# Weighted sums of two key tiles behind each other, and a ring of twelve exponential tiles

## The reference

```
# layer 0: attention in windows of 7 x 7, 8 heads, then two group norms and an MLP
h = relu(group_norm(x + window_cosine_attn(x)))
z = relu(group_norm(h + mlp(group_norm(h))))
# layer 1: attention over all 3136 pixels of an image, 4 heads of 16 channels
q, k, v = split(w_qkv @ z)                       # (64, 3136) each
attn = softmax(q^T k * 16**-0.5)                 # 3136 x 3136 for each head
out  = w_proj @ (attn @ v) + z
```

## Time and profile before

| | |
|---|---|
| median of 3 runs | 9738.71 us (9733.52 to 9741.51) |
| span of the profiled execution | 9740.2 us |
| TensorE busy | 9165.8 us, 94% |
| VectorE busy | 7533.6 us, 77% |
| ScalarE busy | 6369.1 us, 65% |
| one image of the loop, first weigh to first weigh (ninth to tenth image) | about 590.5 us |
| mean granted TensorE clock | 0.965 of full speed |

### The profile page before, as it was taken

How to read it: one execution, slowest core, us unless ns; L and a number is a source line. 1 busy time by engine, 2 the same in 40 slices (tenths; PEclk the granted TensorE clock), 3 DMA queues, 4 the chain that set the end, 5 groups by cost and what they waited for, 6 DMA issues and landing times.

```text
span 9740.2 us, 219440 instructions
## 1 busy us (share of the span) xinstructions
PE 9165.8 (94%) x69126; PEld 3498.0 (36%) x69126; DVE 7533.6 (77%) x9622; ACT 6369.1 (65%) x13874; POOL 837.5 (9%) x676
## 2 busy tenths in 40 slices
PE   4799999999999999999999999999999999999997
PEld 2233333333333333333333333333333333333332
DVE  3687787878878788787877878788787887878784
ACT  1367666666666667666676666667666676666776
POOL 3100100001000000101001000000000001010000
PEclk7799999999999999999999999999999999999999
DMA  1201102020110201102011020201102011020100
GB/s 29 43 8 22 29 9 41 7 37 15 22 28 6 43 9 21 29 5 45 7 24 27 11 38 7 37 15 22 28 6 44 9 21 29 5 45 7 29 14 16
DMA packets 122602, 216.05 MB, mean 22 GB/s; under 512 B 57218, under 2 KB 89090, under 8 KB 121354
## 3 DMA queue, kind: packets, MB, share of 16 engines
q1 hardware_dynamic: 121490, 201.52, 11.6%
HBM read 67.50 MB, written 42.73 MB: 11 GB/s over the span
## 4 chain that ended last, share of the span: by engine, by line
PE 82%; DVE 5%; SPq 4%; DMA 4%; issue 2%; ACT 2%; POOL 1%; DVEq 0%; ACTq 0%; POOLq 0%
PE PS L1353 24%; PE PS L1342 22%; PE PS L1205 21%; PE PS L1244 4%; DVE small L988 3%; PE PS L1264 2%; SPq L716 2%; DMA x_in<-in_x 1%; PE PS L1296 1%; ACT exps L926 1%; PE PS L1253 1%; PE PS L1305 1%; DMA scratch_att<-o_st 1%; PE PS L1275 1%; PE PS L1234 1%
## 5 line engine op out<-in xcount | busy, mean ns | idle before, releaser
L926 ACT ACTIVATE exps<-PS 128x392 f32<-128x392 f32 x12800 | 5566.3, 500 | 2792.0 <-PE PS L1342 2577.2
L988 DVE TENSOR_REDUCE small<-PS 128x1 f32<-128x784 f32 x6400 | 5938.2, 968 | 1056.6 <-PE PS L1205 1010.6
L1342 PE MATMUL PS<-q_stack,k_stack 99*128 99x392 bf16 x12800 | 3525.3, 334 | 50.1 <-ACT exps L926 40.3
L1205 PE MATMUL PS<-k_stack,q_stack 96*128 96x392 bf16 x12800 | 3153.7, 335 | 117.0 <-DVE small L988 45.3
L1353 PE MATMUL PS<-exps,v_all 128*32 128x392 f32 x25600 | 2813.3, 512 | 50.4 <-DVE o_st L1148 41.0
L1342 PEld LDWEIGHTS PS<-q_stack,k_stack 99*128 99x128 bf16 x12800 | 1188.5, 98 | 2439.2 <-ACT exps L926 1649.2
L1205 PEld LDWEIGHTS PS<-k_stack,q_stack 96*128 96x128 bf16 x12800 | 1043.7, 98 | 1677.9 <-DVE small L988 791.7
L1353 PEld LDWEIGHTS PS<-exps,v_all 128*32 128x32 f32 x25600 | 510.1, 108 | 1030.7 <-issue 594.1
L826 POOL TENSOR_TENSOR win_scores<-win_scores,small 128x784 f32<-128x784 f32 x256 | 385.2, 1505 | 3780.9 <-DVE small L1039 3780.9
L1244 PE MATMUL PS<-kmask,tok_unit 113*64 113x392 f32 (+1 forms) x2048 | 407.0, 521 | 16.6 <-DMA tok_unit<-in_query_ident 9.2
L1027 DVE TENSOR_REDUCE small<-PS 128x16 f32<-128x784 f32 x256 | 248.4, 970 | 216.3 <-PE PS L1244 214.5
(11 more groups left out here) (113 smaller groups left out, 3140.1 us busy)
## 6 DMA issues: line engine op xcount, KB each, us to landing
q_stack<-tok_qk SPq DMA_DIRECT2D x320, 98.0 KB, 3.5
k_stack<-tok_qk SPq DMA_DIRECT2D x320, 98.0 KB, 4.2
kmask<-tok_unit SPq DMA_DIRECT2D x1024, 12.2 KB
att<-scratch_att SPq DMA_DIRECT2D x68, 196.0 KB
z_half<-scratch_z SPq DMA_DIRECT2D x34, 392.0 KB, 5.9
inv_sums<-scratch_rden SPq DMA_DIRECT2D x272, 49.0 KB, 2.1
out<-inv_sums SPq DMA_DIRECT2D x68, 196.0 KB, 2.7
scratch_att<-o_st SPq DMA_DIRECT2D x512, 26.0 KB
```

The costliest lines, as they stand in the source:

```text
L926: nc.scalar.activation(exps(u), PS[:, u % SCORE_BANKS, 0:GTOK], ACT.Exp, scale=D1 ** -0.5).then_inc(s_exps, 1)
L988: nc.vector.tensor_reduce(max_parts[:, n_:n_ + 1], slot(), op=ALU.max, axis=AX.XY)\
L1205: last = mm(PS[:, it.bank + j, 0:GTOK], q_stack[0:STACK, stage // 2, tile * 128:(tile + 1) * 128], k_stack[0:STACK, stage // 2, chunk * GT ...
L1342: mm(PS[:, u % SCORE_BANKS, 0:GTOK], k_stack[0:STACK + SHIFT, h, kt * 128:(kt + 1) * 128], q_stack[0:STACK + SHIFT, h, c * GTOK:(c + 1) * ...
```

## The change

The ring of exponentials gets 12 places, 3 quads, and the waits for a free place follow. In the planner a weigh of an odd key tile gets rank 0 as soon as it can go; one of an even key tile may go only when 8 units are scored beyond it, has rank 5 then, and rank 0 from 11 on. The last tile of a stage (number 24) is handled like the even ones. Three planner constants move by a little. Nothing is computed in another way, and the same instructions are issued.

```diff
-EXP_RING = 8
+EXP_RING = 12
...
-    "score": (("PE", 17),), "exp": (("ACT", 41),), "weigh": (("PE", 69),),
+    "score": (("PE", 17),), "exp": (("ACT", 41),), "weigh": (("PE", 68),),
...
-SWITCH, TILED, URGENT = 9, ("weigh", "sum", "wscore", "wpv", "wproj", "qk", "wval", "mlp1", "mlp2", "gqk"), 7
+SWITCH, TILED, URGENT = 10, ("weigh", "sum", "wscore", "wpv", "wproj", "qk", "wval", "mlp1", "mlp2", "gqk"), 11
...
-            needs[at("exp", u)].append((at("weigh", u // 4 - 2), None))
+            needs[at("exp", u)].append((at("weigh", u // 4 - EXP_RING // 4), None))
...
-                rank = 0 if self.scored - 4 * self.weighed >= URGENT else 5
+                tile = step.i % TILES
+                if tile % 2:
+                    rank = 0
+                elif tile == TILES - 1 or self.scored - 4 * self.weighed >= 8:
+                    rank = 0 if self.scored - 4 * self.weighed >= URGENT else 5
+                else:
+                    continue
...
-                    act.wait_ge(s_pv_done, b * QUADS + u // 4 - 1)
+                    act.wait_ge(s_pv_done, b * QUADS + u // 4 - EXP_RING // 4 + 1)
```

## The result

The changed kernel takes 10,450.88 us (median of 4 runs, 10,438.43 to 10,462.36), the kernel before 9740.11 us in the same comparison. The ratio is 1.0734 with a 95% interval of 1.0721 to 1.0747: 7.3% slower. The forecast was 2.5% slower, 9978 us, with a range of 9680 to 10,270. The side was right, the size was not, and the time lies outside the range.

The account below looks back on a forecast made before the run. PE's own work was taken as the bound. A loop image, -5.3 + 6.5 + 15.3 + 2 - 4 = +14.5 us, gives +218 over fifteen; the last image adds 21: +239, so 9978 us, range 9680 to 10,270.

Parts of the forecast that it names:

- PE's own work sets the time: Whole kernel before the change: TensorE busy 94% of the span, almost nothing ending late for it; a quad repeats every 2.24 us.
- Joining saves 0.24 us a pair, 5.3 us an image: Touching weighs on PE: fewer entries to and exits from the column form, 5.3 us less a loop image, 0.7 in the last.
- The ring is worth nothing: Exponential ring of twelve places instead of eight: no gain alone, as ACT hardly waited for a weigh; it only allows the pair.
- Pairs away from layer 0, +0.136 us a quad: Quads without layer 0: PE waits for banks and slots after pairs, 6.5 us more a loop image, 22 in the last.
- Pairs among layer 0 cost nothing: Quads mixed with layer 0: waits 0.19 us a quad before, 0.20 after; taken as nothing, upper end 0.136 a quad.
- R3: Rival: everything starves; pairs among layer 0 wait too, 15 us an image, and stage ends lower PE's clock; 10,310 us, chance 0.25.
- Maxima fall behind: Ends of stages 1 and 3: overdue maxima delay the shift, 15.3 us an image, plus 2 at units 500 and 600.
- The clock: Stage ends: waits send TensorE to its low clock, 7 us more an image; counted only in a rival of chance 0.25.
- The queue: Shift load on SyncE: taken as 2.4 us, with no term for transfers ahead of it and no word on unit 700.
- A wait that goes, -4 us: Start of stage 5: the weigh's 2.7 us wait for DVE's copy and the low clock after it vanish, -4 us a loop image.

Follow-up runs that it names:

- half of both: Old order, changed order with the maxima kept up, and all pairs joined, each with maxima and exponentials over half the columns: 570.0, 570.4, 576.7 us a loop image.
- the maxima kept up: Changed kernel with one planner rank altered, a max behind its rate getting rank 0 instead of 1: 10,008.49 us, ratio 1.0280 to the kernel before.
- the first experiment: Changed kernel with stage 7's shift load moved in SyncE's queue ahead of the stack transfers of heads 1 and 2: 10,200.45 us, ratio 1.0477 to the kernel before.

## Why the prediction was right or wrong

**PE's own work sets the time: right for the kernel before.** With half of both, the three orders come within 0.03 us of what PE's own steps add up to for a quad away from layer 0, and the sign of the forecast came from what the others can't buffer.

**Joining saves 0.24 us a pair, 5.3 us an image: right.** Where two weighs touch, the second starts 0.686 us behind the first (333 times in the changed kernel, 22 in each loop image), and the pair with its exit takes 1.460 us against 1.69, so 0.23 are saved. The parts were read less well than the sum: 1.39 came from halving 2.78 us that were taken at the lower clock, and that came out 0.07 too short; the weigh with a wpv behind it had the 0.69. The same holds for the exponentials: four in 1.78 us are not one in 0.385, as a wait is in them; two in a row take 0.89 below, which is 0.39 apart.

**The ring is worth nothing: right** (1.0001).

**Pairs away from layer 0, +0.136 us a quad: right in the last image, too small in a loop image.** The last image is 23.4 us longer, the forecast was 21. A quad takes 0.154 more. In the last 30 quads of a loop image, with the queue's 15.7 us taken off, it is some 0.2. The half in which the weighs have one max between them, in the changed kernel's last image:

```profile
10104.49 0.87 PE L1359 MATMUL PS<-exps,v_all 128*32 128x392 f32 x8
10105.29 0.51 PE L1211 MATMUL PS<-k_stack,q_stack 96*128 96x392 bf16 x2
10105.73 0.87 PE L1359 MATMUL PS<-exps,v_all 128*32 128x392 f32 x8
...
10106.91 0.89 ACT L932 ACTIVATE exps<-PS 128x392 f32<-128x392 f32 x2 [1.59 <-PE PS L1348]
```

W, M, W start 0.80 and 0.44 apart, and two scores follow; ACT has stood idle for 1.59 us, against 0.46 before. Nothing is saved at a weigh, and ACT has lost 1.1 us that it must make good.

**Pairs among layer 0 cost nothing: wrong, the second step that failed.** I had laid one stretch of 14 quads on the intervals and found 0.20 us of waits a quad against 0.19, with ACT's and DVE's work for layer 0 put in as lumps. Repaired of its maxima and its late load, the changed order was still 17.0 us a loop image slower, where the forecast had 6.5 for pairs away from layer 0 and nothing else of this kind. By quad 170 it had lost 11.3 us in spite of some 3 saved by its 12 touching pairs. With some 3 us for the quads of this part that are free of layer 0, about 11 us are left for the pairs among layer 0; this is an estimate from these figures. The runs with half of both take the 17.0 down to 0.4, so waits for exponentials and maxima carry it in net. R3 named this, at 15 us, and gave it a quarter. The upper end that I had named (0.136 a quad here too) was nearer than zero. Why the laid-out stretch missed these waits was not taken apart.

**Maxima fall behind: right in place and mechanism.** The two stage ends are there, with holes of 14.7 and 15.0 us between scores where I had laid out 13.5 from the first maximum on. Forecast 15.3 + 2 us of loss. The kernel with the early load and the one with the maxima kept up differ by 12.0; with the ten joined pairs more that the first has, it is about 14.

**The clock: in R3 and not in the sum.** The granted clock is at its lower level for 1159 us of the changed kernel against 675 before, in 97 stretches against 56. In the kernel with the maxima kept up it is 685 us in 55. The stretches that begin at the three large holes add up to 556 us, so the added 484 us lie there. Part of the holes' price is this; for the hole at unit 700 it can be at most the 33 us by which the first experiment gave more than the wait. The rule that I had cited from the Trainium skill ("TensorE: Matmul & The Clock Gate", section Loop structure matters more than you think) bears on that hole: the trace agrees, with PE idle for 14.54 us and a clock of 0.77 in the 7 us behind it. In the hole at unit 200 the clock fell as well (0.76 over the window above), while PE was busy for 15.1 of 20 us and stood idle for 1.57 us at the longest.

**The queue: the first step that failed, and the largest.** The forecast followed PE, DVE and the time of the load, and took its 2.4 us as if SyncE were free. It looked at the stage ends at units 200, 400, 500 and 600 and had no word on unit 700, whose transpose stands nine units ahead of the end. SP's order is the same in both kernels at this place. But what matters is when the transfers ahead of the load start, and that moved with layer 0 from 636 scored units to 672. This is 15.7 of the 30 us a loop image by which the forecast was short; the pairs among layer 0 are most of the rest. No rival had the queue either, so the time came out above R3's 10,310 too.

**A wait that goes, -4 us: it is gone, and the size is plausible.** The changed kernel has no recorded wait for `o_st`, and between weighs 123 and 127 it wins 4.7 us on the kernel before, with all else that changed there. Alone, in the kernel before, its removal gave 1.6 to 2.9 us a loop image, as the group norm was waited for instead.

In sum, for a loop image, forecast and measured, where the measured parts are put together from the differences above: joining -5.3 and about -5; pairs away from layer 0 +6.5 and about +9; pairs among layer 0 nothing and about +11; stage ends with the wait that goes +13.3 and about +14; queue nothing and +15.7; total +14.5 and +44.7. That the side was right is not luck, since the foreseen losses are there; but they make up less than half of what was lost.

## What to carry to other kernels

Bringing two long steps together on the engine that sets the time starves its neighbours for that time, and the work made up afterwards needs stores as deep as the gap; here three banks and two slots bridged one weigh and not two, so a saving of 0.23 us a pair cost more than it gave. When an order changes, look at each queue for what is now ahead of a short, urgent transfer, also where that queue's own order is the same. And when two stores may be the cause, shorten the work behind each and behind both: with one alone the other one's wait takes its place.

## What the runs showed that was not expected

With both halves taken off, the changed order was no slower than the old one, but either half alone gave back only 10 of the 37 us between its full and its half-of-both loop image. I had expected one store to be the cause and the other to be slack.

A single maximum rank in the planner moved a loop image by 27.7 us, more than joining 96 pairs could save (22 us).
